# A second router whose logits are summed from x transposed ahead and from the gated rows times the product of the output and router weights

## The reference

```python
x = x + ssm(layernorm(x))        # state space scan, 16 states
x = x + ffn(layernorm(x))        # mixture of 8 experts, first use
x = x + conv(layernorm(x))       # gated long convolution
x = x + ffn(layernorm(x))        # the same mixture, second use
```

```python
# conv
u = short_conv(x @ w_in + b_in)              # three taps along the tokens
v = u[2] * u[0]
v = long_conv(v, filter) + v * filt_bias
out = (v * u[0]) @ w_out + b_out
# ffn
logits = x @ Wr + br                          # x is the normalized input
gate, idx = max(softmax(logits)), argmax(logits)
pos = place of the token among those of its expert, over all tokens in order
out = gate * expert[idx](gate * x) for tokens with pos < 512, else 0   # relu(x W1 + b1) W2 + b2
```

## Time and profile before

| what | value |
|---|---|
| median of 3 runs | 469.01 us (466.15 to 469.39) |
| the profiled execution's own time | 466.43 us |
| its span (first to last instruction) | 464.6 us |
| mean granted clock of TensorE | 0.85 of full speed |
| TensorE busy | 350.6 us, 75% |
| VectorE busy | 333.3 us, 72% |
| GpSimd busy | 290.2 us, 62% |
| ScalarE busy | 232.9 us, 50% |

### The profile page before, as it was taken

The page is one execution under the profiler, slowest core; times in us unless marked ns, Lnnn a source line. Parts: engine busy times, 40 slices in busy tenths (PEclk is TensorE's granted clock), DMA queues, the critical chain, the costliest instruction groups (busy, mean ns, idle before and its releaser), DMA issues.

```text
span 464.6 us, 5440 instructions
## 1 busy us (share of the span) xinstructions
PE 350.6 (75%) x1552; PEld 178.2 (38%) x1552; DVE 333.3 (72%) x772; ACT 232.9 (50%) x383; POOL 290.2 (62%) x203
## 2 busy tenths in 40 slices
PE   4988658769967957969574787287899677688792
PEld 3433213315313403424122554135666655344441
DVE  5999999999999999986433765353869845355341
ACT  3888856556556466533121495044796111346440
POOL 3331497999999999955744000867637565426755
PEclk9999968985967888897767799589599998699987
DMA  6214420784100100101313251111302121132201
GB/s 168 83 70 136 137 66 7 231 309 128 45 0 2 45 1 1 45 4 39 98 36 107 80 161 69 46 34 37 89 0 65 41 79 60 35 126 80 64 15 33
DMA packets 28826, 33.37 MB, mean 72 GB/s; under 512 B 5357, under 2 KB 20737, under 8 KB 28796
## 3 DMA queue, kind: packets, MB, share of 16 engines
q1 hardware_dynamic: 24428, 25.96, 18.0%
q0 software_dynamic: 3712, 6.84, 4.8%
q10 hardware_dynamic: 656, 0.21, 0.2%
HBM read 14.23 MB, written 19.65 MB: 73 GB/s over the span
## 4 chain that ended last, share of the span: by engine, by line
issue 26%; PE 26%; DVE 26%; ACT 9%; another core or an unknown queue 4%; DMA 3%; DVEq 3%; POOL 1%; ACTq 0%; SPq 0%; POOLq 0%
DVE states L786 14%; PE ps L1834 2%; ACT scaled L1393 2%; PE ps L1920 2%; PE ps L1345 2%; PE ps L1073 2%; PE ps L1613 2%; DVE scratch L482 2%; PE ps L153 2%; PE ps L1191 2%; PE ps L1329 1%; PE ps L1909 1%; ACT ps L780 1%; POOL x L1289 1%
## 5 line engine op out<-in xcount | busy, mean ns | idle before, releaser
L924 POOL TENSOR_TENSOR states<-states,c_rows 128x1024 f32<-128x1024 f32 x60 | 142.6, 2410 | 9.2 <-DVE dtu L503 5.1
L786 DVE TENSOR_TENSOR_SCAN states<-ps,inp 128x1024 f32<-128x1024 f32 x64 | 140.5, 2264 | 0.6 <-ACT ps L780 0.5
L780 ACT ACTIVATE ps<-ps,bias_p,scale_p 128x1024 f32<-128x1024 f32 x64 | 75.0, 1177 | 57.0 <-PE ps L774 57.0
L1165 POOL DMA_INDIRECT slots<-x,put x56 | 54.7, 977 | 43.8 <-DVE put L1159 28.8
L774 PE MATMUL ps<-stack,sel 96*128 96x512 bf16 x128 | 47.7, 466 | 28.9 <-DVE states L786 27.4
L1289 POOL DMA_INDIRECT x<-answers,put x28 | 27.3, 976 | 50.8 <-DMA answers<-reply 39.6
L1488 POOL DMA_INDIRECT out<-reply,home x32 | 31.8, 995 | 23.5 <-DVE reply L1465 15.9
L1465 DVE SCALAR_TENSOR_TENSOR reply<-ps,rows,kept 128x128 f32<-128x128 f32 x64 | 18.6, 344 | 26.4 <-remote 12.0
L808 PE MATMUL ps<-states,red 128*32 128x512 f32 x256 | 36.2, 673 | 0.2 <-POOL states L924 0.2
L774 PEld LDWEIGHTS ps<-stack,sel 96*128 96x128 bf16 x128 | 9.7, 107 | 64.8 <-DVE states L786 54.2
L1861 DVE SCALAR_TENSOR_TENSOR c_s<-c_u,c_w_tap,c_s 128x1024 f32<-128x1024 f32 (+1 forms) x20 | 20.6, 1068 | 13.0 <-ACT c_s L1851 11.4
(11 more groups left out here) (207 smaller groups left out, 675.7 us busy)
## 6 DMA issues: line engine op xcount, KB each, us to landing
slots<-zero SPq DMA_DIRECT2D x8, 528.0 KB
rows<-slots SPq DMA_DIRECT2D x16, 264.0 KB
steps<-part SPq DMA_DIRECT2D x4, 768.0 KB, 3.3
stack<-steps SPq DMA_DIRECT2D x12, 256.0 KB, 4.1
answers<-x SPq DMA_DIRECT2D x4, 512.0 KB, 3.2
answers<-reply SPq DMA_DIRECT2D x8, 256.0 KB, 3.2
out<-x SPq DMA_DIRECT2D x3, 512.0 KB
x<-in_x SPq DMA_DIRECT2D x4, 256.0 KB, 3.1
```

What stands on the lines that cost most here:

```text
L780: act.activation(bank(ps, slot(b, u), 2), bank(ps, slot(b, u), 2), ACT.Exp, scale=m["scale_p"][:, group(u):group(u) + 1], bias=m["bias_p"] ...
L786: dve.tensor_tensor_scan(h[:, u * SEQ:(u + 1) * SEQ], bank(ps, slot(b, u), 2), inp[:, b * SEQ:(b + 1) * SEQ], 0.0, ALU.mult, ALU.add).then ...
L924: eng.tensor_tensor(h[:, u * SEQ:(u + 1) * SEQ], h[:, u * SEQ:(u + 1) * SEQ], c_rows[:, b * SEQ:(b + 1) * SEQ], ALU.mult).then_inc(done, 1)
L1165: pool.indirect_dma_start(out=m["slots"][n // BATCH], out_offset=bass.IndirectOffsetOnAxis(m["put"][:, b, i:i + 1], 0), in_=m["x"][:, b * ...
```

## The change

The logits of the second router are (x + bias + z w_out) w_r for each token, with z the gated rows c_z. The changed kernel sums them in two parts in one PSUM bank: `input_logits` multiplies x with its bias, transposed before the output is added to it, by w_r; `output_logits` multiplies z, which is already transposed, by `w_route` = w_out w_r. The product w_out w_r is made once, by a transposition of w_out, a matmul (`route_tensor`, which borrows part of z's buffer) and two copies on ScalarE. `to_router` now waits for `biased`, not `x_done`, and the places of the transpositions, of ScalarE's copies and of the logits in the hand-written lists move. `gate_y` of batch b waits for the logits of batch b - 2 (they read z's buffer), and `add` waits for the transpositions of x. There are 32 more matmuls with 8 columns. `logit` only names a slice.

```diff
--- before.py
+++ after.py
@@ -1063,15 +1063,24 @@
         self.tr.transpose(pe, "r", n, self.m["x"][:, b * BT:(b + 1) * BT, 0:D], ready, count)
 
     def copy(self, act, n):
-        need(act, self.logit_psum, n - BATCH - 1)
         self.tr.copy(act, "r", n, self.m["rx_t"][:, n % 2, :])
 
-    def logits(self, pe, n):
+    def logit(self, i=0, tiles=1):
+        at = self.LOGITS * HALF + i * EXPERTS
+        return self.ps[:, at:at + tiles * EXPERTS]
+
+    def input_logits(self, pe, n):
+
         self.tr.need_copy(pe, "r", n)
         need(pe, self.logit_read, n - BATCH)
         for i in range(BT):
-            last = pe.matmul(self.ps[:, self.LOGITS * HALF + i * EXPERTS:self.LOGITS * HALF + (i + 1) * EXPERTS],
-                             self.m["rx_t"][:, n % 2, i * P:(i + 1) * P], self.m["w_r"][:, :], start=True, stop=True)
+            pe.matmul(self.logit(i), self.m["rx_t"][:, n % 2, i * P:(i + 1) * P], self.m["w_r"][:, :], start=i == 0, stop=False)
+
+    def output_logits(self, pe, n, z, z_done, w):
+
+        need(pe, z_done, n - BATCH + 1)
+        for i in range(BT):
+            last = pe.matmul(self.logit(i), z[:, i * P:(i + 1) * P], w[:, :], start=False, stop=i == BT - 1)
         last.then_inc(self.logit_psum, 1)
 
     def choose(self, dve, n):
@@ -1087,7 +1096,7 @@
             dve.tensor_tensor(m["logit"][:, :, :], m["row_logit"][:, n, :].rearrange("p (i e) -> p i e", e=EXPERTS), spread_out, ALU.mult)
         else:
             dve.wait_ge(self.logit_psum, n - BATCH + 1 + CREDIT)
-            dve.tensor_tensor(m["logit"][:, :, :], bank(self.ps, self.LOGITS)[:, 0:BT * EXPERTS].rearrange("p (i e) -> p i e", e=EXPERTS),
+            dve.tensor_tensor(m["logit"][:, :, :], self.logit(0, BT).rearrange("p (i e) -> p i e", e=EXPERTS),
                               spread_out, ALU.mult).then_inc(self.logit_read, 1)
         dve.drain()
         dve.tensor_tensor(m["logit"][:, :, :], m["logit"][:, :, :], same(m["b_r"][:, :]), ALU.add)
@@ -1666,6 +1675,7 @@
         self.xn, self.xt = sb("c_xn", [P, 2, SEQ]), sb("c_xt", [P, 2, SEQ])
         self.u = sb("c_u", [P, 2, 2, self.PAD + SEQ])
         self.s, self.v, self.vt, self.z = sb("c_s", [P, 2, 2, SEQ]), sb("c_v", [P, 2, SEQ]), sb("c_vt", [P, 2, SEQ]), sb("c_z", [P, 2, SEQ])
+        self.w_route = sb("c_w_route", [P, EXPERTS])
         self.weights_in, self.taps_out, self.taps_in = plan.dma_sem("c_weights_in"), plan.dma_sem("taps_out"), plan.dma_sem("taps_in")
         self.cleared, self.v_done, self.biased = plan.sems("gpsimd", "c_cleared c_v c_biased")
         self.mlp_psum, self.flip_psum, self.u_psum, self.y_psum, self.o_psum = plan.sems(
@@ -1740,6 +1750,12 @@
         pe.wait_ge(self.taps_in, 16)
         pe.matmul(self.ps[:, 5 * HALF:5 * HALF + 2 * P], self.m["const"][:, C_FLIP:C_FLIP + P], self.flipped[:, :], start=True,
                   stop=True).then_inc(self.flip_psum, 1)
+        pe.transpose(self.ps[:, 6 * HALF:6 * HALF + P], self.w_out[:, :], self.m["const"][:, C_ID:C_ID + P]).then_inc(self.flip_psum, 1)
+
+    def route_tensor(self, pe):
+        need(pe, self.toep_done, 2)
+        pe.matmul(self.ps[:, 6 * HALF + P:6 * HALF + P + EXPERTS], self.z[:, 0, 0:P], self.m["w_r"][:, :], start=True,
+                  stop=True).then_inc(self.flip_psum, 1)
 
     def filter_abs(self, act):
         act.wait_ge(self.weights_in, self.n_weights)
@@ -1757,6 +1773,10 @@
     def toeplitz_scalar(self, act):
         need(act, self.flip_psum, 1)
         act.copy(self.toep[:, :], self.ps[:, 5 * HALF:5 * HALF + 2 * P]).then_inc(self.toep_done, 1)
+        need(act, self.flip_psum, 2)
+        act.copy(self.z[:, 0, 0:P], self.ps[:, 6 * HALF:6 * HALF + P]).then_inc(self.toep_done, 1)
+        need(act, self.flip_psum, 3)
+        act.copy(self.w_route[:, :], self.ps[:, 6 * HALF + P:6 * HALF + P + EXPERTS]).then_inc(self.toep_done, 1)
 
     def filter_vector(self, dve):
 
@@ -1923,10 +1943,11 @@
         if halves[-1]:
             last.then_inc(self.y_psum, 1)
 
-    def gate_y(self, dve, b):
+    def gate_y(self, dve, b, routed):
         q = b % 2
         need(dve, self.y_psum, b + 1)
         need(dve, self.o_psum, b - 1)
+        need(dve, routed, b - 1)
         dve.tensor_tensor(self.z[:, q, :], bank(self.ps, self.Y, 2), self.s[:, q, 0, :], ALU.mult).then_inc(self.z_done, 1)
 
     def output(self, pe, b):
@@ -1940,6 +1961,7 @@
         x = self.m["x"][:, b * BT:(b + 1) * BT, 0:D]
         need(dve, self.o_psum, b + 1)
         need(dve, self.biased, b + 1)
+        need(dve, self.tr.full, self.tr.at("r", BATCH + b))
         dve.tensor_tensor(x, x, by_tile(bank(self.ps, self.OUT, 2)), ALU.add).then_inc(self.x_done, 1)
         dve.drain()
 
@@ -1947,8 +1969,8 @@
 def mixtures_and_conv(plan, ps, m, t):
     late_memory(plan, m, t)
 
-    order = [("c", 0), ("v", 0), ("c", 1), ("r", BATCH), ("c", 2), ("v", 1), ("c", 3), ("v", 2), ("r", BATCH + 1), ("v", 3),
-             ("r", BATCH + 2), ("r", BATCH + 3)]
+    order = [("c", 0), ("r", BATCH), ("v", 0), ("c", 1), ("r", BATCH + 1), ("c", 2), ("v", 1), ("c", 3), ("r", BATCH + 2), ("v", 2),
+             ("r", BATCH + 3), ("v", 3)]
     tr = Transposer(plan, ps, m, order)
     router = Router(plan, ps, m, tr)
     experts = Experts(plan, ps, m, router)
@@ -2017,25 +2039,32 @@
         need(pe, experts.reply, experts.tiles(EXPERTS - 1))
         conv.toeplitz_tensor(pe)
         keep_clock(pe, m, ps, 1, 8)
+        conv.route_tensor(pe)
         conv.transpose_first(pe, 1)
         conv.streams(pe, 0, 1)
 
         def to_router(b):
-            router.transpose(pe, second(b), conv.x_done, b + 1)
-
+            router.transpose(pe, second(b), conv.biased, b + 1)
+
+        def from_conv(b):
+            router.output_logits(pe, second(b), conv.z[:, b % 2, :], conv.z_done, conv.w_route)
+
+        to_router(0)
         pe.wait_ge(conv.u_done, conv.stream(0, 1, 1) + CREDIT)
-        keep_clock(pe, m, ps, 0, 8)
+        keep_clock(pe, m, ps, 7, 8)
         pe.wait_ge(conv.s_first, conv.twice(0, 1, 1) + CREDIT)
-        keep_clock(pe, m, ps, 0, 8)
+        keep_clock(pe, m, ps, 7, 8)
         conv.v_transpose(pe, 0)
         conv.open_conv(pe, 0)
+        need(pe, conv.toep_done, 3)
+        router.input_logits(pe, second(0))
         conv.long_conv(pe, 0)
         conv.transpose(pe, 1)
         conv.output(pe, 0)
         conv.streams(pe, 1, 0)
         conv.streams(pe, 1, 1)
-        to_router(0)
-        router.logits(pe, second(0))
+        from_conv(0)
+        to_router(1)
         need(pe, conv.u_done, conv.stream(1, 1, 1))
         keep_clock(pe, m, ps, conv.U, 6)
         conv.transpose(pe, 2)
@@ -2049,26 +2078,27 @@
         conv.streams(pe, 3, 0)
         conv.output(pe, 1)
         conv.streams(pe, 3, 1)
+        to_router(2)
         conv.v_transpose(pe, 2)
         conv.open_conv(pe, 2)
-        to_router(1)
+        router.input_logits(pe, second(1))
+        from_conv(1)
+        to_router(3)
         conv.long_conv(pe, 2)
-        router.logits(pe, second(1))
         conv.output(pe, 2)
         conv.v_transpose(pe, 3)
         router.count(pe, second(1))
-        to_router(2)
+        router.input_logits(pe, second(2))
+        from_conv(2)
         conv.open_conv(pe, 3)
-        router.logits(pe, second(2))
         conv.long_conv(pe, 3)
         router.count(pe, second(2))
+        router.input_logits(pe, second(3))
         need(pe, conv.u_done, conv.stream(BATCH - 1, 1, 1))
         keep_clock(pe, m, ps, conv.U, 3)
         conv.output(pe, 3)
-        keep_clock(pe, m, ps, conv.U, 6)
-        to_router(3)
-        router.logits(pe, second(3))
-        keep_clock(pe, m, ps, conv.U, 5)
+        from_conv(3)
+        keep_clock(pe, m, ps, conv.U, 8)
         router.count(pe, second(3))
         keep_clock(pe, m, ps, conv.U, 6)
         late.turn_rows(pe, 0)
@@ -2122,6 +2152,7 @@
         conv.copy(act, 0, (1,))
         conv.take_streams(act, 0, 1)
         conv.first_tap(act, 0, 1)
+        router.copy(act, second(0))
         conv.v_copy(act, 0)
         conv.deviations(act, 1)
         conv.normalize(act, 1)
@@ -2129,8 +2160,8 @@
         conv.take_streams(act, 1, 0)
         conv.deviations(act, 2)
         conv.take_streams(act, 1, 1)
-        router.copy(act, second(0))
         conv.first_tap(act, 1)
+        router.copy(act, second(1))
         conv.normalize(act, 2)
         router.row_deviations(act, second(0))
         conv.copy(act, 2)
@@ -2144,16 +2175,15 @@
         conv.copy(act, 3)
         conv.take_streams(act, 3, 0)
         conv.take_streams(act, 3, 1)
+        router.copy(act, second(2))
         conv.v_copy(act, 2)
         conv.first_tap(act, 3)
+        router.copy(act, second(3))
         router.row_deviations(act, second(1))
-        router.copy(act, second(1))
         router.probabilities(act, second(1))
         conv.v_copy(act, 3)
-        router.copy(act, second(2))
         router.row_deviations(act, second(2))
         router.probabilities(act, second(2))
```

(9 more changed lines are left out.)

## The result

The changed kernel takes 472.94 us (median of six runs, 470.94 to 479.65), the kernel before 466.81 us (six runs, 465.37 to 469.39): ratio 1.0096, 95% interval 1.0057 to 1.0134. The ratio is estimated from the executions in the usual, faster state (the one of 479.65 us is not among them) and is not the quotient of the two medians. The change makes the kernel about 1% slower, and the time lies above the range that was given. The profiled execution took 473.14 us, with a span of 471.3 us.

A forecast was written before the change was run, and what follows sets the result against it. The chain of waits through the second router's convolution stage was taken as the bound, GpSimd next. Clock +1.9 and tail -5.4 (including -1.0) sum to -3.5: 462.9, say 463.0 us; own range 460 to 466, with rivals 457.5 to 470.0.

The forecast's parts named there:

- behind it all of batch 3 hangs on this `put`, as before: After batch 3's `put`: count, dense expert, row loads and experts wait for it, so the tail's -5.4 us passes on.
- late ends: Near 380 and 393 us VectorE starts 3.15 and 3.66 us after TensorE's rows end, unexplained.
- Set-up at nothing: At 287 to 290 us: making w_out w_r costs nothing, or 0.5 us if ScalarE's copies came on the path.
- Input logits of batch 0 and the clock behind, together +1.9: Up to batch 2's streams near 336 us: logits ahead of long_conv(0) cost 0, half of a 1.2 GHz doubling +1.9.
- 353 to 379 us, term -1.0: TensorE queued without a break at full clock: batch 3's long convolution 1.0 us earlier; ends -2.0 and +3.4.
- All the extra matmuls of this stretch are thus paid by the idle time before 370 us: In 353 to 379 us: TensorE's former idle time, waiting for batch 2's addition, covers the added matmuls; term -1.0.
- rival C: Slower: low clock in the stretch where TensorE is queued, 353 to 379 us, and at the streams; 471.3 us, chance 0.13.
- L1093 at 0.1 instead of 2.5: VectorE's choice at 367.2 us: L1093 comes after GpSimd's product ends, so costs 0.1 us, where it took 2.51.
- The tail: From batch 3's long convolution: choice starts at 390.4 instead of 396.32, -5.9 us; -5.4 passes on to the last scatter.
- rival B: Gain not there: last logits' late end was chance, or lands on another group; 3.4 us fewer, 466.4 us, chance 0.27.
- rival A: Convolution tail: no late ends, GpSimd bound and scattering without a pause; -8.1 us, 458.3 us, chance 0.18.
- theory M: From the experiments, on the turns near 398 us: the late end comes at its moment whatever TensorE has queued; 1.008 to 1.014.

The follow-up runs named there:

- f4: Kernel before with the change for batch 3 alone, set-up included, input_logits(3) behind output(3): ratio 0.9992 to the kernel before.
- e4: Changed kernel without the eight fillers behind the output logits of batch 3: ratio 1.0079 to the kernel before.
- e1: Kernel before plus 64 tiny matmuls that nobody reads, in TensorE's idle time near 290 us: ratio 1.0005.
- g5: f4 with x(3) transposed between output(2) and v_transpose(3), input_logits(3) ahead of output(3): 0.9911 to the kernel before; repeated on a chip without late ends, 0.9986.
- f0: The changed kernel itself, run again beside the kernel before: ratio 1.0115.
- f1: Changed kernel with input_logits(1), output_logits(1) and to_router(3) moved behind long_conv(2): ratio 1.0066 to the kernel before.
- g2: Changed kernel with input_logits(3) behind output(3): 0.9994 to the kernel before; repeated on a chip without late ends, 1.0115.
- g7: Changed kernel with batch 1's logits and batch 3's transposes behind long_conv(2), input_logits(3) behind output(3), input_logits(0) behind long_conv(0): 1.0053 to the kernel before.
- g8: Kernel before with 32 added matmuls of 128x8, read by nobody, between to_router(1) and long_conv(2): ratio 1.0114.
- e3: Changed kernel without the six fillers behind the dense path's transposes: ratio 1.016 to the kernel before, four executions only.

## Why the prediction was wrong

Forecast were 463.0 us and a gain of 3.5; measured is a loss of 6.1 by the medians and 6.7 by the profiled executions. The forecast adds the +1.9 of the early part to the whole, so it has the last scatter at 400.81 - 3.5 = 397.3 us, and its times for the middle and the tail are to be read with 1.9 added. The last scatter came at 399.08. Of the 10.2 us between -3.5 and +6.7, 1.8 stand there, 7.8 between it and the first reply, and 0.7 behind.

Two steps failed. In the profiled execution it is "behind it all of batch 3 hangs on this `put`, as before", a term that was put at nothing and was 7.8 us. On the chips without late ends it is the term for 353 to 379 us, put at -1.0 at full clock, from which a loss comes. Point by point:

- *Set-up at nothing*: right within the noise (f4 0.9992 with it).
- *Input logits of batch 0 and the clock behind, together +1.9*: measured is 1.3 us at v's transposes of batch 1 (341.67 against 340.36), by the mechanism given: the streams took 5.67 us, where 3.95 + 1.9 was forecast. Without late ends it was 0.3 us (c_z of batch 1 342.10 in e4, 341.76 in e1).
- *353 to 379 us, term -1.0*: failed. The order of the groups was right, and with 1.3 us from the early part long_conv(2) starts where it was forecast (362.1 and 363.37). But then I held the clock at full: long_conv(2) took 1.7 us more, open_conv(3) 1.0 and long_conv(3) 0.8. Its row ends at 383.27, 3.7 us later than before; without the 1.3 the term was +2.4 and not -1.0, inside the other end of +3.4 "if the clock falls". "All the extra matmuls of this stretch are thus paid by the idle time before 370 us" is wrong even at full clock: in e4 long_conv(3) starts 1.4 us later than in e1. The low clock is rival C's mechanism, which had 0.13 and 471.3 us. That its number comes near the measured time is luck: these rows make 3.5 us of C's 8.3, and most of the loss in this execution is behind the scatters.
- *L1093 at 0.1 instead of 2.5*: right (0.23), and the rule of the Trainium skill on who interferes with whom (SBUF — State Buffer) is borne out twice, by this row and by the instruction beside GpSimd's product, which took 2.68 us in e1 and takes 0.66 in e4, where less of it falls beside the product.
- *The tail*: right in kind, and near in place by luck. The choice starts at 393.02, where the forecast with its +1.9 has 392.3. But the late ends are not where it let them stand: 0.9 us at c_z and not 3.15, none at the last logits where it had 3.57, and one of 3.5 at the count of batch 2, which it didn't have (row's end 383.49). `place` of batch 2 waited for that signal and the addition stood behind it. The last scatter starts directly behind the one before, as forecast, but 1.8 us later (399.08 and 397.3), since `put` of batch 2 is 2.6 us later than before (388.53 and 385.91). With an untouched middle the tail's term exists: g5's choice is 7.8 us earlier than before, of which 1.1 us stand at c_z of batch 0 already.
- *"Behind it all of batch 3 hangs on this `put`, as before"*: failed. Last scatter to first reply took 12.7 us before and takes 20.5. The late end at the turns and the low clock behind it make the dense path end last. This is what rival B called "lands on another group", priced at 3.4 us, and on a group that I had not looked at. On the chips without late ends it fails in another way: the end hangs on `put` of batch 2, and GpSimd scatters without a pause. That is what rival A described, and it holds for the order of before too (e1).

The balance of the profiled executions: -1.7 us at the last scatter and +7.8 behind it make the +6.0 at the first reply. Without late ends the balance is another one, +1.4 us from `put` of batch 2 to the end and the executions with the low clock, and the ratio is still 1.008 to 1.009 (1.006 to 1.014 with fillers taken out). What both have in common is a TensorE that gets four groups of 1.8 us more, has two groups of logits ahead of long_conv(2) where it had none, and meets its low clock there in some executions. No run took only these two groups away on a chip without late ends. That the two ratios agree may be chance.

Open: what makes the late ends, and what decides the group that they fall on. In the traces with them, one of 1.3 to 7.4 us begins between 392.7 and 400.6 us in every kernel (before, after, f0, f1, f4, g2, g5, g7, g8), on the logits, the count or the turns, whichever is there. That would fit theory M, but no run tested it, and it is weaker than it looks: the same traces have late ends in both mixtures too, so one in this stretch is no sign of a fixed moment. In the kernel before, VectorE waits 4.48 us for one before 250.50 and 7.34 us before 444.57, both marked "remote".

## What to carry to other kernels

Taking a transpose off the last path doesn't pay if the work that replaces it goes ahead of an operation that the other engine already waits for; put it where TensorE idles, and only for the batch whose wait it removes, not for all (g5, which gained 0.9% on one chip and lost nothing on another). A stretch in which TensorE is queued without a break has to be costed at 1.2 GHz as well, and before a gain is passed on to the end, every path that starts beside the last one has to be followed too: here the end hung on the dense path in one trace and on the scatter of the batch before in others, and not on the last `put`. A gain that is made of an unexplained wait must be measured on more than one chip.

## What the hardware showed beyond that

- The same kernel takes 466.8, 470.7 and 470.7 us on some chips and 444.9, 445.2 and 445.0 us on others. On the first, signals of TensorE come late behind the end of their rows, up to 7.6 us in the convolution stage (g7, x's transposes, row's end 325.57 and copy at 333.15); on the others none comes over 0.6 us late. Until the scan ends they run alike (the last scan at 196.7 us in before and in e1); the first mixture's last `put` is at 240.1 and 230.2, the first reply of the second mixture at 413.54 and 398.83, and the time from there to the end is 51.1 and 44.4 us. So the chips part in the stages in which late ends stand. The mean granted clock is 0.850 and 0.871 for before and e1.
- Where they occur, they are no noise of one execution: the changed kernel has 3.5 us at count(2) and 7.4 us at the turned rows on one chip, 3.6 and 7.1 us on another.
- Taking out TensorE's fillers behind the turns (e3) left TensorE idle for 1.5 us ahead of L1622 and gained nothing.
